# Attention output computed already transposed, with denominators by their own matmuls

## The reference

```python
q = rope(ln(x) @ Wq); k = rope(ln(x) @ Wk); v = ln(x) @ Wv      # 32, 8, 8 heads of 128
scores = einsum('bkgqd,bkmd->bkgqm', qg, k) / sqrt(128)          # 4 query heads per KV head
attn = softmax(where(causal, scores, -inf))
out = einsum('bkgqm,bkmd->bkgqd', attn, v)
x = x + out @ Wo
h = ln(x)
gates = softmax(top2(h @ Wr.T))                                  # 4 experts
x = x + sum_e gates_e * 16/sqrt(16) * (h @ A_e.T) @ B_e.T
```

## Time and profile before

| | us |
|---|---|
| Median of 2 runs | 4264.63 (4260.18 to 4269.07) |
| Profiled execution | 4274.17 |
| Its span on the slowest core (core 4) | 4272.6 |
| TensorE matmul busy | 3197.8 (75%) |
| VectorE (DVE) busy | 1046.7 (24%) |
| ScalarE (ACT) busy | 1011.1 (24%) |
| Mean granted TensorE clock | 0.868 |

### The profile page before, as it was taken

One profiled execution on the slowest core, in us unless ns is written; L12 is line 12 of the kernel. 1 busy time (PEld: TensorE's weight loads), 2 busy tenths in 40 slices (PEclk: granted clock), 3 DMA queues, 4 the chain that ended last, 5 costly groups with the idle time before them and its releaser, 6 DMA issues.

```text
span 4272.6 us, 45702 instructions; the slowest of 8 cores (4251.7 to 4272.6 us)
## 1 busy us (share of the span) xinstructions
PE 3197.8 (75%) x17204; PEld 1524.1 (36%) x17520; DVE 1046.7 (24%) x2421; ACT 1011.1 (24%) x1109; POOL 72.5 (2%) x86
## 2 busy tenths in 40 slices
PE   3666776766437998789529998879736999877983
PEld 2222223222213444434214444444313444444441
DVE  3111106000342223300352222210243221211015
ACT  2000005000212004700220007820122003984002
POOL 0000000000000000000000000000000000000000
PEclk9888887888758999999659999989857999998995
DMA  7999991898334551044044550034223552002431
GB/s 164 180 175 188 200 191 37 185 179 179 87 138 137 170 173 68 21 158 148 29 177 146 173 167 24 1 110 156 89 118 133 169 177 84 1 1 89 148 118 79
DMA packets 215704, 530.63 MB, mean 124 GB/s; under 512 B 82112, under 2 KB 168256, under 8 KB 169408
## 3 DMA queue, kind: packets, MB, share of 16 engines
q1 hardware_dynamic: 53280, 421.72, 27.5%
q0 software_dynamic: 87456, 84.97, 15.0%
q10 hardware_dynamic: 74752, 20.99, 2.3%
HBM read 474.19 MB, written 117.44 MB: 138 GB/s over the span
## 4 chain that ended last, share of the span: by engine, by line
PE 54%; DMA 19%; ACT 11%; DVE 10%; issue 5%; DVEq 0%; ACTq 0%; SPq 0%; POOLq 0%
PE pd L293 44%; ACT epair L585 8%; DMA wblk<-wq 5%; DMA wblk<-wo 5%; DMA wscr<-wblk 4%; DVE bst L341 4%; PE pd L620 3%; PE pd L326 3%; PE pd L561 2%; ACT xnhn L357 2%; DMA wblk<-wscr 2%; DMA h<-x 1%; DVE epair L597 1%; DMA wblk<-wk 1%; DMA wblk<-wv 1%
## 5 line engine op out<-in xcount | busy, mean ns | idle before, releaser
L293 PE MATMUL pd<-xnT,wblk 128*128 128x512 bf16 x5016 | 1157.7, 391 | 157.4 <-DMA wblk<-wq 121.4
L293 PE MATMUL pd<-wblk,aoT 128*128 128x512 bf16 x4012 | 922.8, 391 | 153.2 <-DMA wblk<-wo 111.7
L293 PEld LDWEIGHTS pd<-xnT,wblk 128*128 128x128 bf16 x5120 | 511.2, 100 | 803.0 <-issue 240.1
L585 ACT ACTIVATE epair<-pd,cvals 128x1024 bf16<-128x1024 f32 x544 | 629.2, 1200 | 322.2 <-PE pd L561 282.0
L293 PEld LDWEIGHTS pd<-wblk,aoT 128*128 128x128 bf16 x4096 | 408.8, 100 | 666.3 <-issue 213.2
L620 PE MATMUL pd<-vaug,epair 128*128 128x129 bf16 x4352 | 356.4, 222 | 162.1 <-ACT epair L585 93.4
L326 PE MATMUL pd<-iden,xnhn 128*128 128x128 bf16 x1024 | 137.9, 303 | 416.9 <-ACT xnhn L357 324.0
L620 PEld LDWEIGHTS pd<-vaug,epair 128*128 128x128 bf16 x4352 | 266.0, 98 | 415.1 <-issue 408.9
L374 DVE TENSOR_TENSOR t1b<-qswp,sing 128x512 bf16<-128x512 bf16 x160 | 110.8, 692 | 1069.2 <-DMA qswp<-qt 898.8
L703 DVE TENSOR_TENSOR h<-pd,h 128x512 f32<-128x512 f32 x128 | 79.5, 684 | 1002.8 <-PE pd L293 1002.8
L465 ACT ACTIVATE qt<-pd 128x512 bf16<-128x512 f32 x128 | 76.4, 597 | 1032.7 <-PE pd L293 985.9
(11 more groups left out here) (58 smaller groups left out, 916.3 us busy)
## 6 DMA issues: line engine op xcount, KB each, us to landing
wblk<-wscr SPq DMA_DIRECT2D x240, 1024.0 KB, 5.2
wscr<-wblk SPq DMA_DIRECT2D x80, 1024.0 KB, 8.0
h<-x SPq DMA_DIRECT2D x24, 2048.0 KB, 9.7
wblk<-wq POOLq DMA_DIRECT2D x32, 1024.0 KB, 14.5
wblk<-wo POOLq DMA_DIRECT2D x32, 1024.0 KB, 13.8
out<-h SPq DMA_DIRECT2D x16, 2048.0 KB, 6.3
qswp<-qt ACTq DMA_DIRECT2D x256, 64.0 KB, 4.8
wblk<-wk POOLq DMA_DIRECT2D x8, 1024.0 KB, 13.5
```

Of the source, the lines that this page charges most:

```text
L293: nc.tensor.matmul(o, l, r, start=st, stop=sp))
L585: nc.scalar.activation(epair[p][:, 0:ncols], src, AF.Exp, bias=cvals[:, 3:4], scale=cvals[:, 2:3]))
```

## The change

P·V is turned around. V (128x128) is the stationary operand and the probabilities of four heads (512 columns) the moving one, so that a chain ends with [dim, query], the form the output projection needs. V's column of ones is not used any more. The denominators come from a second matmul per step, with a 128x1 column of ones as stationary operand, into one row of bank 6. At the end of a chain DVE takes the reciprocal of that row (1x512, bf16 result), TensorE spreads it over 128 partitions by a matmul with a 1x128 row of ones into bank 7, DVE copies that to SBUF (in xnhn) and multiplies the P·V bank by it straight into aoT. P·V uses banks 4 and 5 in turn. attn_out and its transposes are gone. aoT is now written while qt is still read, so the arenas change: h0, h1 share with qt, and xnT, aoT, hnT share arena1.

```diff
-    h = [at("h0", [128, c.D], F32, arena1_off),
-         at("h1", [128, c.D], F32, arena1_off + TLB),
+    h = [at("h0", [128, c.D], F32, qtar_off),
+         at("h1", [128, c.D], F32, qtar_off + TLB),
...
-    aoT = at("aoT", [128, c.NCH * c.GROUP_T], BF16, qtar_off)
-    hnT = at("hnT", [128, c.NCH * c.GROUP_T], BF16, qtar_off)
+    aoT = at("aoT", [128, c.NCH * c.GROUP_T], BF16, arena1_off)
+    hnT = at("hnT", [128, c.NCH * c.GROUP_T], BF16, arena1_off)
...
-                for g4 in range(4):
-                    w2 = [eready[ix], ("V", vaug_ready[k][i])]
-                    bank = pvb[g4 // 2]
...
-                    tv2 = sch.T(w2, lambda e, b=bank, p=p, mi=mi, g4=g4, k=k, i=i, jg=jg:
-                                nc.tensor.matmul(
-                                    b.ap[:, (g4 % 2) * 129:(g4 % 2) * 129 + 129],
-                                    epair[p][:, mi * 512 + g4 * 128:
-                                             mi * 512 + (g4 + 1) * 128],
-                                    vaug[:, (i * c.NHKV + k) * 129:
-                                         (i * c.NHKV + k) * 129 + 129],
-                                    start=(i == 0 and g4 % 2 == 0),
-                                    stop=(i == jg and g4 % 2 == 1)))
...
+                tvp = sch.T(w2, lambda e, b=pvb, p=p, mi=mi, slot=slot, i=i, jg=jg:
+                            nc.tensor.matmul(
+                                b.ap[:, 0:512],
+                                vaug[:, slot:slot + 128],
+                                epair[p][:, mi * 512:(mi + 1) * 512],
+                                start=(i == 0), stop=(i == jg)))
+                w3 = [eready[ix], ones_ready] + (dnb.readers if i == 0 else [])
+                tvd = sch.T(w3, lambda e, p=p, mi=mi, r=dnr, i=i, jg=jg:
+                            nc.tensor.matmul(
+                                dnb.ap[r:r + 1, 0:512],
+                                ones_m[:, :],
+                                epair[p][:, mi * 512:(mi + 1) * 512],
+                                start=(i == 0), stop=(i == jg)))
...
                 if i == jg:
...
+                            return nc.vector.reciprocal(
+                                rden[0:1, :], dnb.ap[r:r + 1, 0:512])
+                    rv = sch.V([("T", tvd), ("T", rden_last[0])], _recip)
+                    dnb.readers.append(("V", rv))
+                    wb = [("V", rv), ones_ready] + bcb.readers
+                    bcb.readers = []
+                    tbc = sch.T(wb, lambda e: nc.tensor.matmul(
+                        bcb.ap[:, 0:512], ones1[:, :], rden[0:1, :],
+                        start=True, stop=True))
...
+                    vcp = sch.V([("T", tbc)] + wrb, lambda e: nc.vector.tensor_copy(
+                        xnhn[:, 0:512], bcb.ap[:, 0:512]))
...
+                    vv = sch.V([("T", tvp), ("V", vcp)] + wa,
+                               lambda e, d=dst, b=pvb: nc.vector.tensor_tensor(
+                                   d, b.ap[:, 0:512], xnhn[:, 0:512], OP.mult))
...
-            for cq, vv in transpose_tile(
-                    attn_out[jl], aoT, jl,
...
             if jl < 2:
-                xdma[jl] = sch.X(wts, lambda e, r=row0, jl=jl:
+                xdma[jl] = sch.X(wts + [("A", qt_w_last[0])],
+                                 lambda e, r=row0, jl=jl:
                                  e.dma_start(h[jl][:, :], x_d[r:r + 128, :]))
```

More of the change, by code:

```diff
@@ L188, in build_program @@
     hextra_off = place(2 * TLB)
-    h = [at("h0", [128, c.D], F32, arena1_off),
-         at("h1", [128, c.D], F32, arena1_off + TLB),
+    assert c.NHKV * 4 * c.GROUP_T * 2 == 2 * TLB
+    h = [at("h0", [128, c.D], F32, qtar_off),
+         at("h1", [128, c.D], F32, qtar_off + TLB),
          at("h2", [128, c.D], F32, hextra_off),
          at("h3", [128, c.D], F32, hextra_off + TLB)]
-    attn_out = [at(f"ao{j}", [128, c.D], BF16, arena1_off + j * c.D * 2)
-                for j in range(c.GT)]
     xnT = at("xnT", [128, c.NCH * c.GROUP_T], BF16, arena1_off)
     qt = at("qt", [128, c.NHKV * 4 * c.GROUP_T], BF16, qtar_off)
-    aoT = at("aoT", [128, c.NCH * c.GROUP_T], BF16, qtar_off)
-    hnT = at("hnT", [128, c.NCH * c.GROUP_T], BF16, qtar_off)
+    aoT = at("aoT", [128, c.NCH * c.GROUP_T], BF16, arena1_off)
+    hnT = at("hnT", [128, c.NCH * c.GROUP_T], BF16, arena1_off)
     wblk = [at(f"wblk{i}", [128, 8 * 512], BF16) for i in range(2)]
@@ L226, in build_program @@
     arcp = at("arcp", [128, 4], F32)
+    ones_m = at("ones_m", [128, 1], BF16)
+    ones1 = at("ones1", [1, 128], BF16)
+    rden = at("rden", [1, 512], BF16)
     cvals = at("cvals", [128, 4], F32)
@@ L258, in build_program @@
     ts_last = [0]
+    qt_w_last = [0]
+    rden_last = [0]
+    rbc_last = [0]
     gate_last = [0]
@@ L395, in build_program @@
     wc2 = sch.W([], lambda e: e.dma_start(bcat[:, :], bcat_d[:, :]))
-    ones_ap = vaug[:, :].rearrange("p (s v) -> p s v", v=129)[:, :, 128:129]
-    vo = sch.V([], lambda e, a=ones_ap: nc.vector.memset(a, 1.0))
+    sch.V([], lambda e: nc.vector.memset(ones_m[:, :], 1.0))
+    vo = sch.V([], lambda e: nc.vector.memset(ones1[:, :], 1.0))
+    ones_ready = ("V", vo)
     sch.V([], lambda e: nc.vector.memset(cvals[:, 0:1], EPS))
@@ L432, in build_program @@
             rg_hs[slot].use("A", a3s[-1])
-            warena = (rg_hs[0].take(("xnT", g)) + rg_hs[1].take(("xnT", g))) if jl == 0 else []
+            warena = rg_qtar.take(("xnT", g)) if jl == 0 else []
             for cq, vv in transpose_tile(xnhn, xnT, jl,
@@ L462, in build_program @@
                 dst = qt_head(s, hh)
-                wq0 = rg_qtar.take(("qt", g)) if (s == 0 and hh == 0) else []
+                wq0 = (rg_hs[0].take(("qt", g)) + rg_hs[1].take(("qt", g))) \
+                    if (s == 0 and hh == 0) else []
                 a1 = sch.A([("T", bank.writer)] + wq0,
@@ L466, in build_program @@
                                d, b.ap[:, 0:512], AF.Identity))
+                qt_w_last[0] = a1
                 bank.readers.append(("A", a1))
@@ L552, in build_program @@
         NSTEP = len(steps)
-        attn_ready = [[0] * c.NHKV for _ in range(c.GT)]
+        aoT_blk_ready = [[] for _ in range(nblk)]
         def emit_scores(idx):
@@ L571, in build_program @@
         pvb = None
+        dnr = 0
+        dnb = psum[6]
+        bcb = psum[7]
         first_exp = True
@@ L632, in build_program @@
-                if i == jg:
[L633 to L661, removed]
-            for cq, vv in transpose_tile(
-                    attn_out[jl], aoT, jl,
[L664 to L668, removed]
+                slot = (i * c.NHKV + k) * 129
@@ new lines, in build_program @@
+                w2 = [eready[ix], ("V", vaug_ready[k][i])]
+                if i == 0:
+                    w2 = w2 + pvb.readers
+                    pvb.readers = []
+                tvp = sch.T(w2, lambda e, b=pvb, p=p, mi=mi, slot=slot, i=i, jg=jg:
[4 more added lines that the diff above has]
+                                start=(i == 0), stop=(i == jg)))
@@ new lines, in build_program @@
+                w3 = [eready[ix], ones_ready] + (dnb.readers if i == 0 else [])
[5 more added lines that the diff above has]
+                                start=(i == 0), stop=(i == jg)))
+                rg_ebuf[p].use("T", tvd)
+                rg_ropescr.use("T", tvd)
@@ new lines, in build_program, with _recip @@
+                if i == jg:
+                    pvb.writer = tvp
+                    dnb.writer = tvd
+                    def _recip(e, r=dnr):
+                        with nc.allow_low_precision(reason="bf16 softmax recip"):
+                            return nc.vector.reciprocal(
[7 more added lines that the diff above has]
+                        start=True, stop=True))
+                    bcb.writer = tbc
+                    rden_last[0] = tbc
+                    wrb = rg_xnhn.take(("rbc", g)) + [("V", rbc_last[0])]
+                    vcp = sch.V([("T", tbc)] + wrb, lambda e: nc.vector.tensor_copy(
+                        xnhn[:, 0:512], bcb.ap[:, 0:512]))
+                    bcb.readers.append(("V", vcp))
+                    wa = rg_qtar.take(("aoT", g))
+                    dst = aoT[:, 4 * k * c.GROUP_T:(4 * k + 4) * c.GROUP_T] \
+                        .rearrange("p (a t) -> p a t", t=c.GROUP_T)[
+                        :, :, jl * 128:(jl + 1) * 128]
+                    vv = sch.V([("T", tvp), ("V", vcp)] + wa,
+                               lambda e, d=dst, b=pvb: nc.vector.tensor_tensor(
+                                   d, b.ap[:, 0:512], xnhn[:, 0:512], OP.mult))
+                    pvb.readers.append(("V", vv))
+                    rbc_last[0] = vv
+                    rg_xnhn.use("V", vv)
+                    rg_qtar.use("V", vv)
+                    if jl == c.GT - 1:
+                        aoT_blk_ready[min(k // 2, nblk - 1)].append(("V", vv))
@@ L669, in build_program @@
+        rg_hs[0].use("T", sch.cnt["T"])
```

(1 more changed line is left out.)

17 lines of the change are left out of this document (4 added, 13 removed).

## The result

The changed kernel is slower: 1.207 times the time of the kernel before, 95% interval 1.201 to 1.214. The forecast was slower by 16%, 4936 us within 4430 to 5100; the runs took 5138 to 5200 us, the profiled one 5159.9 (its span 5158.3 us on core 7).

A forecast was written before the change was run, and what follows sets the result against it. The prediction took the loop exponential, P·V, scores, exponential to bound attention, with neither TensorE nor ScalarE full. Attention +759 us (clock +168 included) and transposes -87 gave +672: 4936 us, slower by 16%, range 4430 to 5100.

The forecast's parts named there:

- The sign and the main mechanism: At each chain's end, TensorE's broadcast waits for DVE's reciprocal with score matmuls queued behind; overall slower by 16%.
- R: Time of DVE's 1x512 reciprocal at a chain's end, taken as 3.2 us from a slope of 6 ns an element.
- the cases with a slow reciprocal: Cases where the chain-end reciprocal takes 3.2 us or more: main 4936 us (30%), 5070 (22%), 4768 (20%), and beyond (2%).
- Rival (a): Chain-end reciprocal at one element per cycle, 0.69 us, and the clock stays: 4447 us; chance 22%.
- (c): Chain-end reciprocal repeats still more steps per element, 8 ns each, 4.25 us in all: 5070 us; chance 22%.
- the pair, 1.46 us: Period of a pair of attention steps, up from 1.25 us, with four 512-column matmuls at 0.217 us: +114 us.
- (d): Denominator matmuls cost no time of their own beside P·V and the reciprocal takes 0.69 us: 4340 us; (d) and less 4%.
- rival (b): Slow reciprocal at each chain's end, but TensorE's clock stays: 4768 us; chance 20%.
- The clock's price: TensorE's idle at each chain's end lowers its clock: 1.5 us a chain, 144 for 96 chains plus 24 in group 0, +168 us.
- Transposes and loads: Stretches between attention and output projection: transposes go, but 16 us of loads stay in each of groups 1 to 3; -87 us.
- The exchange of the arenas: New sharing of buffers at group boundaries costs nothing; if cover were gone, one store of 6.3 us exposed three times.
- The link as the bound of attention: In attention, the loop exponential, P·V, scores, exponential sets 2.50 us per two pairs before the change, 2.92 after.

The follow-up runs named there:

- the kernel with full ones: Against the changed kernel, denominator matmuls use 128x128 ones instead of 128x1, with results in all 128 partitions of bank 6; 5036 us, a single run.
- the fillers: Against the changed kernel, 14 matmuls that nobody reads put ahead of each chain's broadcast matmul; 4922 and 4927 us, ratio 1.154.
- The kernel with all three taken away: Against the changed kernel: 128x128 ones into banks 6 and 7 in turn, reciprocal over 128 partitions, no broadcast; 4390 to 4404 us, ratio 1.030.
- the two prefetching kernels: Two projection weight blocks loaded before h0, h1; against changed kernel's out-of-loop form, 4174 to 4194 us; against earlier kernel with scores two pairs ahead, 4122 to 4141.

## Why the prediction was wrong, point by point

**The sign and the main mechanism were right.** Scores stand behind the waiting broadcast, so the reciprocal's length goes into the time 128 times. DVE to TensorE and back took what was worked out: 3.60 us of idle against 3.5.

**R was right in size, and partly by luck.** It is 3347 ns against the 3.2 us taken. The slope of 6 ns an element came out at 6.2 (3347 less 164, over 511). But 6 ns was the difference of 164 and a median of 170, and the rows with two elements lie anywhere from 148 to 172; by their mean the slope would have been negative:

```profile
L639 DVE RECIPROCAL arcp<-pd 128x2 f32<-128x2 f32 x256 | 30.4, 160 | 90.4 <-PE pd L620 86.9 <-PE pd L326 2.9 <-issue 0.2
```

The prediction called these differences weak, and gave the cases with a slow reciprocal three quarters of its chances all the same. Rival (a), one element a cycle, is out, and so is (c) with its R of 4.25, although its 5070 is of all the cases the nearest to the measured time. The Trainium skill's repeat count of 8 ("VectorE: DVE Perf Modes", section "Walkthrough: the 8-slice pipeline in each mode") would have given an estimated 4.4 us; the measured row stands, and it is shorter by a quarter.

**The term that failed is the pair, 1.46 us.** The step reads: four matmuls of 512 columns at 0.217. The pitch came from a stage in which every stationary operand is 128x128, and it was carried over to one where 128x128 and 128x1 alternate. There each matmul costs 0.31, four of the six in a pair, and 1.69 us of TensorE overtake the link of 1.46 as the bound. With full ones two pairs take 2.90, 1.45 each, so the rest of this term was right. Over 544 pairs that is 0.23 x 544 = 125 us; the kernel with full ones gives them back (5036 against about 5160), and 134 by the stages (1617.2 against 1750.9). The prediction did name a pitch other than 0.217 as what would make it wrong, but gave it no case and no end of the range; only a gain was considered there (d).

**The clock's price was too low.** The mechanism was right and rival (b), that the clock stays, is out. The price was 1.5 us a chain from weight-bound stages and 24 in group 0, 168 us; with the fillers 237 us come back, or 227 by the stages: 2.0 a chain in groups 1 to 3, and 34 in group 0. What the forecast had too short is the time at the low level. These windows are of the stage of the earlier trace rows in the kernel before:

```profile
610.48:614.00 3.52, 3.52 (x9) 1.31 (x10) 0.00 (x0) 0.00 (x0) 0.00 (x0) 0.52 1.14 132
614.00:619.20 5.20, 5.15 (x24) 2.15 (x22) 0.00 (x0) 0.00 (x0) 0.00 (x0) 1.00 1.09 292
```

And this one is of the chain's end above in the changed kernel:

```profile
4615.00:4621.00 6.00, 5.86 (x13) 1.19 (x13) 1.38 (x2) 1.41 (x2) 0.00 (x0) 0.54 0.00 0
```

In the stage that gave the price the low level lasted about 3.4 us behind an idle of 4.24; in attention it lasts 5.0 on average behind 3.60. A pair takes 2.96 us there (from the start of its scores at 4616.71 to that of the next at 4619.67) and 1.69 at 2.4 GHz, so 43% of that time is lost, an estimated 2.1 us, which is what the stages show. TensorE has hardly any idle time of its own in this stretch (5.86 of 6.00 us busy). Why the low level lasts longer in attention isn't settled.

The terms account for what is missing. The excess of attention over the forecast is 950 - 759 = 191 us. The pitch gives 125 to 134, the clock 227 or 237 less 168, which is 59 to 69, and R another 0.15 x 128 = 19, 203 to 222 together. That it is somewhat too much is to be expected if the pitch and the clock overlap, since a visible load costs more at 1.2 GHz and the kernel with full ones gets that part back as well; this is argued, and no run shows the overlap by itself. The kernel with all three taken away comes to within 40 us of what was expected of it.

**Transposes and loads** were right: -81 against -87, with 19.7, 18.3 and 17.0 us in place of 16. h0 and h1 do stand ahead of the first weight block, and the two prefetching kernels show that this order was the whole of that wait. The exchange of the arenas cost next to nothing, as taken: from the start of the output projection to the next attention stage the changed kernel takes 7.2 and 2.2 us more and 0.7 less.

**The link as the bound of attention** was right for the kernel before, as that kernel with scores two pairs ahead shows. This reading of the earlier trace rows was worth more than the change: it gives 2.7% in one edit.

The range ended at 5100 because its upper end varied the reciprocal's length alone. Beside it stood two more terms: the pair, whose excess is about a seventh of the whole effect, was varied downwards only, and the clock, about a quarter of it, was priced from a stage of another kind.

## What to carry to other kernels

- A pitch read from one stage holds for the same shapes in the same order. When an edit alternates stationary operands of different shape, price the weight load as visible, about 0.1 us a change here, or give the small operand the full 128 columns: that was 2.4% of this kernel (one run), and it also makes the broadcast unnecessary.
- An engine that waits in the middle of its queue costs its wait, the latency both ways and what its clock loses behind it. Here 3.35 us on DVE in one row cost 3.60 us of idle and some 1.85 us of low clock, and dummy matmuls in the hole gave 4.6% back.
- Before a stage's operations are exchanged, find the loop that sets its period. Here moving work out of that loop was worth more than the new data layout.

## What the runs showed of the hardware

- A reciprocal on DVE took 3347 ns for 1x512 and 3358 for 128x512, 6.5 ns an element of the free dimension, whether it has one partition or 128. A cast of the same row took 680.
- Weight loads of 128x128 behind 128x128 were hidden (0.21 to 0.22 us from start to start at 512 columns); from 128x128 to 128x1 and back they weren't (0.31 at 2.4 GHz, 0.51 to 0.57 at 1.2). The Trainium skill ("TensorE: Matmul & The Clock Gate", section "Step-by-step: what each phase is for") says that a weight load is pulled ahead of matmuls in flight if the row groups don't conflict or if it goes to the background buffer. That agrees with the uniform case; that passage names no exception for a change in the number of columns, and the rows here show one.
- In attention of groups 1 to 3 the granted clock stayed at 0.97 to 0.99 with some 0.95 us of idle at each chain's end, and fell to 0.77 to 0.86 with 3.60 us. Matmuls whose result is never read kept it up (1.00 with 14 of them in the hole).
